# A perceiver layer on one core: key weights loaded third on ScalarE's queue, and the attention prologue's evacuations in another order

## What is computed

```python
x = x + xattn(layernorm(x), ctx, ctx)      # sigmoid(qp @ kp.T / sqrt(128)) @ vp, 49 blocks of 512 context rows
x = x + attn(layernorm(x))                 # 16 heads of 32, causal, latent keys/values of 128, rope of 32
x = x + ffn(layernorm(x))                  # 8 experts, the best one by a gate; relu(g)^2 * u, then down
```

## Time and profile before

| what | us |
|---|---|
| median of 3 runs | 577.19 (576.92 to 577.48) |
| the profiled execution | 577.08 |
| its span | 575.3 |
| TensorE busy | 569.4 |
| VectorE busy | 456.4 |
| ScalarE busy | 401.7 |

### The profile page before, as it was taken

One profiled execution on the slowest core, in us unless ns is written; L12 is line 12 of the kernel. 1 busy time (PEld: TensorE's weight loads), 2 busy tenths in 40 slices (PEclk: granted clock), 3 DMA queues, 4 the chain that ended last, 5 costly groups with the idle time before them and its releaser, 6 DMA issues.

```text
span 575.3 us, 8075 instructions
## 1 busy us (share of the span) xinstructions
PE 569.4 (99%) x3010; PEld 477.2 (83%) x3010; DVE 456.4 (79%) x494; ACT 401.7 (70%) x542; POOL 1.7 (0%) x7
## 2 busy tenths in 40 slices
PE   8999999999999999999999999999999999999998
PEld 5888888888888888888888888888888887877887
DVE  6987878787878797889787978787878798887742
ACT  6776767676768687768667877776776784797321
POOL 1000000000000000000000000000000000000000
DMA  8668777768677877777778877767787743000201
GB/s 327 229 199 248 233 237 236 225 221 240 218 220 251 265 244 238 236 255 259 226 246 254 254 227 250 219 221 222 217 275 234 229 142 114 33 1 2 74 1 38
DMA packets 33239, 115.90 MB, mean 201 GB/s; under 512 B 4080, under 2 KB 4784, under 8 KB 32944
## 3 DMA queue, kind: packets, MB, share of 16 engines
q1 hardware_dynamic: 32768, 115.05, 62.7%
q10 hardware_dynamic: 432, 0.33, 0.2%
HBM read 114.84 MB, written 0.52 MB: 201 GB/s over the span
## 4 chain that ended last, share of the span: by engine, by line
PE 92%; ACT 3%; DMA 2%; DVE 2%; issue 1%; DVEq 0%; ACTq 0%; SPq 0%
PE ps L395 44%; PE ps L336 22%; PE ps L354 12%; PE ps L924 4%; PE ps L956 2%; DMA rawn<-in_ctxn 1%; PE ps L813 1%; PE ps L525 1%; ACT w L742 1%; PE ps L722 1%; PE ps L657 1%; PE ps L749 1%; PE ps L606 1%; DMA x_s<-in_x 1%; PE ps L292 1%
## 5 line engine op out<-in xcount | busy, mean ns | idle before, releaser
L395 PE MATMUL ps<-nh,zl 128*128 128x512 f32 x388 | 142.8, 390 | 0.1
L395 PE MATMUL ps<-nh,zh 128*128 128x512 f32 x388 | 142.7, 390 | 0.0
L395 PE MATMUL ps<-nl,zh 128*128 128x512 f32 x388 | 142.5, 389 | 0.0
L369 DVE TENSOR_TENSOR zl<-zf,zh 128x1024 fp32r<-128x1024 f32 x49 | 60.1, 1226 | 79.6 <-ACT zh L368 79.6
L255 DVE TENSOR_TENSOR nl<-rawn,nh 128x1024 fp32r<-128x1024 f32 x96 | 114.0, 1221 | 1.4 <-issue 0.8
L235 DVE TENSOR_TENSOR tl<-rawt,th 128x1024 fp32r<-128x1024 f32 x96 | 113.2, 1218 | 1.8 <-ACT th L230 1.7
L252 ACT ACTIVATE nh<-rawn 128x1024 fp32r<-128x1024 f32 x96 | 99.8, 1057 | 12.3 <-DMA rawn<-in_ctxn 11.1
L230 ACT ACTIVATE th<-rawt 128x1024 fp32r<-128x1024 f32 x96 | 96.3, 1053 | 2.3 <-DMA rawt<-in_ctxt 2.3
L364 ACT ACTIVATE zf<-ps 128x512 f32<-128x512 f32 x98 | 58.2, 597 | 56.3 <-PE ps L354 50.6
L395 PEld LDWEIGHTS ps<-nh,zl 128*128 128x128 f32 x388 | 72.7, 188 | 16.0 <-DVE zl L369 1.0
L395 PEld LDWEIGHTS ps<-nl,zh 128*128 128x128 f32 x388 | 72.9, 188 | 15.2
(11 more groups left out here) (193 smaller groups left out, 618.5 us busy)
## 6 DMA issues: line engine op xcount, KB each, us to landing
rawn<-in_ctxn SPq DMA_DIRECT2D x97, 512.0 KB, 6.4
rawt<-in_ctxt SPq DMA_DIRECT2D x96, 512.0 KB, 4.8
h_s<-in_wg SPq DMA_DIRECT2D x4, 512.0 KB, 6.7
h_s<-in_wu SPq DMA_DIRECT2D x4, 512.0 KB, 6.6
wds<-in_wd SPq DMA_DIRECT2D x4, 512.0 KB, 3.9
raw<-in_ctxt SPq DMA_DIRECT2D x2, 512.0 KB, 8.7
h_s<-in_wvt SPq DMA_DIRECT2D x2, 512.0 KB, 7.6
wq_s<-in_wq SPq DMA_DIRECT2D x1, 1024.0 KB, 10.1
```

The costliest lines, as they stand in the source:

```text
L369: ZL[b] = put("vector", lambda e: e.tensor_tensor(zl[b % 2][:], zf[:], zh[b % 2][:], ALU.subtract), [ZH[b]] + av, "zl")
L395: m = put("tensor", lambda e, z=z, n=n, i=i, j=j, r=r: e.matmul(bank(4 + r), z[:, j * T + r * P:j * T + r * P + P], n, start=(b == 0 and i ...
```

## The change

Five edits:

- ScalarE's queue loads the identity first, the biases second and the key weights third. `wkh` keeps its place among ScalarE's instructions.
- TensorE multiplies zeros 17 times instead of 22.
- In the prologue the four key copies' first half (`k_copies(0, 4, range(2))`) moves behind the evacuation of the second rows and `hqh` on ScalarE, and `rope(0, 2)` behind that evacuation on VectorE.
- `q_copies` takes the list of pieces that go to VectorE: quarter 0 as before (1, 3), quarter 1 only (3,), quarter 2 as before, quarter 3 all four.
- `a_scores` waits for the copies of every quarter that its heads come from, not of the last alone.

```diff
         DX = [dma("sync", x_s[:, r, :], xr[:, r, :], f"dx{r}") for r in range(2)]
-        DWK = dma("scalar", wk_s[:], wkt, "dwk")
         DID = dma("scalar", id_s[:], ident, "did")
         wq0 = zf
         DBK = dma("scalar", bqk_s[:], bqk, "dbk")
+        DWK = dma("scalar", wk_s[:], wkt, "dwk")
...
-        for k in range(22):
+        for k in range(17):
             put("tensor", lambda e: e.matmul(bank(7), wz[:, 0:P], wz[:], start=True, stop=True), [WZ])
...
-        def q_copies(t, bk, mark):
+        def q_copies(t, bk, mark, on_v):
...
-                if i % 2:
+                if i in on_v:
...
-        k_copies(0, 4, range(2))
         HN.append(norm_rows(1, RS[1]))
...
         values_up(0, 6, 1)
-        add = rope(0, 2)
         HT.append([put("vector", lambda e: e.tensor_scalar(hT[:, 0:2, half(1)], chunks(0)[:, 0:2], 2.0, None, ALU.mult),
                        [m[1]], "lne_v"),
                    put("scalar", lambda e: e.activation(hT[:, 2:4, half(1)], chunks(7)[:, 2:4], ACT.Copy, scale=2.0),
                        [m[3]], "lne_a")])
-        f = add()
+        f = rope(0, 2)()
         low_h = split_h(1)
+        k_copies(0, 4, range(2))
         latents(1, 5, 7, 3, 0, [YB[1]])
...
-        q_copies(0, 1, query(0, 1, []))
-        q_copies(1, 5, query(1, 5, []))
+        q_copies(0, 1, query(0, 1, []), (1, 3))
+        q_copies(1, 5, query(1, 5, []), (3,))
...
-            wait = [*QA[heads[-1] // 4], *(m for r in ROT.values() for m in r), KA[0], KA[1], VE[0]] if p else \
-                [*QA[1], *ROT[0], KA[0], VE[0]]
+            quarters = [m for t in range(heads[0] // 4, heads[-1] // 4 + 1) for m in QA[t]]
+            wait = quarters + ([*(m for r in ROT.values() for m in r), KA[0], KA[1], VE[0]] if p else [*ROT[0], KA[0], VE[0]])
...
-        q_copies(2, 2, QT)
+        q_copies(2, 2, QT, (1, 3))
         QT = query(3, 1, QA[0])
         exps(0)
-        q_copies(3, 1, QT)
+        q_copies(3, 1, QT, (0, 1, 2, 3))
```

## The result

Device microseconds, median of the runs (lowest to highest):

| | before | changed |
|---|---|---|
| time | 577.27 (576.92 to 577.48), 6 runs | 581.24 (579.02 to 583.41), 6 runs |
| profiled execution, own time | 577.08 | 580.50 |
| its span | 575.3 | 578.7 |
| its mean granted clock | 1.00 | 0.997 |

A forecast was written before the change was run, and what follows sets the result against it. TensorE was taken to bound the kernel, almost without idle time after 9 us. The sum was 577.08 + 2.46 (late root) + 0.15 (prologue) = 579.7 us, range 578.2 to 581.5.

The forecast's parts named there:

- The place of the loss: Start: the root waits behind wkh on ScalarE, +2.46 us; TensorE, nearly without idle time after 9 us, gives nothing back.
- The landing: ScalarE's load queue: key weights, now third, land at 7.9 us by row-by-row sharing with SyncE's queue; wkh follows.
- The rule of whole packets: Load queues: engines change queues only after 9 to 17 descriptors, so key weights could land at 6.6 us; judged against.
- Fewer dummies: TensorE's start: 17 dummies end at about 6.7 us, nothing gained; the pause before the transposes grows from 0.07 to 3.6 us.
- (a): Rival, 20%: TensorE's clock falls in the longer pause before the transposes, costing 1.7 us: 581.4 us.
- (d): Main case, 60%: late root and prologue loss without a fall of the clock, 578.8 to 580.5 us.
- kr: Prologue: ckv runs 0.48 us later behind the key copies, so kr starts +0.15 us instead of -0.18.
- First scores: Prologue: ScalarE's third copy of quarter 1 makes the last query copy, and the scores following it, +0.17 us later.
- Second scores: Prologue: scores(2) gains some 0.2 us, since ScalarE loses two copies and VectorE's six end at 511.6 us.
- Maxima: Prologue: VectorE's six copies push back unit 1's maxima and evacuation, so unit 2's maxima start +0.18 us later.
- Prologue in all: Net of the reordered rows and copies and the query copies: +0.15 us, between -0.2 and +0.35.
- The base: Starting point of the sum: the profiled execution's own time before the change, 577.08 us (span 575.3 and 1.8 around it).

The follow-up runs named there:

- e1: The changed kernel with the key weights' load back in first place, 17 dummies and the prologue as changed: 577.23 us, ratio 1.0005.
- e2: The kernel before with only the load order changed (key weights third), 22 dummies: 580.77 us, ratio 1.0067.
- e8: The kernel before with the new load order, 17 dummies and wkh on VectorE behind the normalised rows: 577.25 us, ratio 1.0001.
- e9: The kernel before with the new load order, 22 dummies and seven more that wait for wkh: 579.54 us, ratio 1.0038.
- e11: The changed kernel with the key weights loaded first again and each semaphore waited for once ahead of the scores: 576.50 us, ratio 0.9990.
- e10: The changed kernel with wkh on VectorE and each semaphore waited for once before the scores: 576.84 us, ratio 0.9996; one of twelve runs at 1056.17 us left out.
- e12: The kernel before with the new load order, 17 dummies and wkh on ScalarE behind the first half of th: 577.11 us, ratio 1.0006.
- e5: The kernel before with the prologue's edits alone, each semaphore waited for once ahead of the scores: 576.83 us, ratio 0.9991.
- e3: The kernel before with the new load order and 34 dummies instead of 22: 579.90 us, ratio 1.0047.

## Why the prediction was right or wrong

**The place of the loss: right for the late start.** The root behind the waiting wkh carried the start, and the stream gave nothing back; e1 and e2 show it from both sides. But "nothing after 9 us can absorb a later start" left out that the work behind the pause could itself become longer, by 1.46 us up to 14.3.

**The landing: right, 0.15 us too late.** wkh started at 7.75 us, not 7.9. Of the remaining 0.15 us of the start's error, 0.10 has a cause that recurs below: I added durations end to end, but ScalarE starts its next instruction about 0.1 us before the last one's recorded end (the root at 8.28, wkh until 8.38). The other 0.04 is a slip of the sum: 7.9 + 0.63 is 8.53, not 8.57. The rule of whole packets that I had weighed (the Trainium skill, DMA: Bandwidth & Descriptors, Queues, rings and completion order) gave 6.6 us for the landing; 7.75 here, and 7.57 to 9.02 in the runs with this order, speak for the row-by-row sharing. So do the last rows in e8, where one engine is late: 0.235 us apart, against the 0.083 + 0.16 of the sum.

**Fewer dummies: right.** Nothing was gained, and the pause came out at 3.50 us (predicted 3.6). They lengthened it, yet e2, with all 22, lost the clock too. What I should have priced in the main case was the pause itself, and most of that comes from the load.

**The likeliest case: wrong.** The step that failed is the choice between (a) and (d). I counted against a fall that no fall is seen anywhere in the trace, though no pause in that trace was long enough to show one: an absence without an occasion is not evidence. The only long idle time that it did hold is the one ahead of the first dummy, and behind it the dummies went at half pace, 0.43 us apart, which I had read myself ahead of the doubled pace in the earlier trace rows. The Trainium skill (TensorE: Matmul & The Clock Gate, Part 1) says that idleness brings the throttled state back. The traces agree for pauses of 3.50 us (five of six executions) and 2.59 us (three of four), with no fall in the kernels whose profiles show pauses of 0.71 (e9), 0.85 (e11), 0.98 (e10, but for the execution at 0.53) and 1.18 us (e8), and one fall in ten executions of e12. With (a) as the likeliest case the number would have been 581.4, against 581.24 measured. Its price was nearly right, 1.7 against 1.46, since it was taken from the first climb. That the time lies inside the range on record is owed to the room left for (a), not to the case I took.

**kr: direction right, size off.** I had `ckv` 0.48 us later; it came 0.36 later (502.11, less 3.18, against 498.57), again because ScalarE's starts overlap. kr, which could wait 0.37 us for it without harm, moved by -0.01 and not +0.15.

**First scores: +0.41 instead of +0.17, a missing term.** The last copy came only 0.04 us later relative (508.84, less 3.18, against 505.62), better than my 0.17. The other 0.37 us are wait instructions: their number rose from four to six with the change's longer list, and their order turned against it. The list of the change names each semaphore several times, and I had put its waits at nothing. e5 names each once and gets the earlier start that the deal was able to give.

**Second scores: direction right, start wrong. Maxima: right.** scores(2) gained 0.24 on the first scores, by the deal that I had priced at 0.2, but they came 0.17 later than before, not 0.2 earlier: the six copies on VectorE that they wait for began at 509.18 relative, not at 508.94, because the first scores were late. The maxima of unit 2 start at 516.87, which is +0.22 relative (predicted +0.18). Prologue in all +0.24 against +0.15, inside the bounds given.

**The base.** The 0.39 us by which one block of the profiled execution of before was longer stood in the sum as if it were the kernel's; since the median of before's runs lies above that execution all the same, it did the number no harm. The runs' medians differ by 3.97 us, the two profiled executions by 3.42. The changed kernel's executions go with the clock (579.02 at 1.00, 583.41 at 0.994), but the four at 0.997 themselves lie 1.57 us apart, and e3 and e9 scatter as much at 1.00; that part is open.

## What to carry to other kernels

Before a load is put behind others on its queue, ask who consumes it, and what stands behind that consumer on an in-order engine: here a copy of 0.63 us, off the path by 1 us, took the whole start with it. A new pause of TensorE has two prices, its own length and what the clock takes afterwards, and the second is not in the trace of before unless that trace holds such a pause; fill it with work that waits for the same event, not with a fixed number of dummies. When an instruction waits for many signals, name each semaphore once, and look in the trace at which wait is passed last: here it was the one that the list named first.

## What the hardware showed that I had not expected

- The clock does not fall in the pause but after it: in the changed kernel the transposes still keep their pace (the keys follow 1.18 us behind their start, as in e1 with 1.17), and only from 10.9 to 14.3 us does the work go at half pace; e2 shows the same, 0.73, 0.50 and 0.92 from 10 to 16 us.
- The granted clock of the profile does not show the start: it reads 1.00 there, in before too, while the first dummies go at 0.43 us, half the later pace. A 1.00 ahead of the first rise says nothing; the spacing of equal multiplications does.
- The first rise is not fixed either: between 7 dummies at 0.43 us (risen at about 4.1 us, changed kernel and e2) and 15 (at about 7.2 us, e3 and e5) went by before it, though the first dummy starts at 1.31 us in all of them.
- A pure wait of TensorE costs 0.106 us even when its signal is there already, and a row of the profile can name a coincident instruction of another engine as the one waited for (L645 above, with the true one ScalarE's last copy).
- The third load of ScalarE's queue, with the loads ahead of it the same, was taken up at 7.57 (e3), 7.73 (e9), 7.75 (changed kernel), 7.93 (e2), 8.76 (e10) and 9.02 us (e8). In e10 and e8, 15 of the 16 engines' counts are there by 7.59 and 7.41 us; a single engine is late, by another 1.1 and 1.6 us. In the other four and e12 the last count comes between 7.54 and 7.91. Why is open, and so is whether it belongs to these kernels or to these executions.
